# Gathers of a recommendation kernel: one pause ahead of arrival 16, or a pause each ahead of arrivals 16 and 17

## The reference

```
sparse_embed = emb_tables[field, x_sparse]           # 512 x 26 x 64
gram  = einsum('bik,bjk->bij', sparse_embed, sparse_embed)
inner = gram[:, iu, ju]                              # the 325 pairs i < j
dnn_in = concat([x_dense, sparse_embed.reshape(512, 1664), inner])   # 512 x 2002
h   = relu(dnn_in @ w1 + b1)                         # w1 is 2002 x 2002
out = sigmoid(h @ w2 + b2)                           # 512 x 1
```

## Time and profile before

| | us |
|---|---|
| median of 3 runs | 213.66 |
| lowest and highest | 212.72, 214.28 |
| the profiled execution's time | 214.66 |
| its span | 212.5 |
| TensorE busy | 201.6 (95% of the span) |
| VectorE busy | 148.6 (70%) |
| ScalarE busy | 129.3 (61%) |
| GpSimd busy | 129.4 (61%) |
| bytes moved | 39.00 MB, 184 GB/s in the mean |

### The profile page before, as it was taken

How to read it: one execution, slowest core, us unless ns; L and a number is a source line. 1 busy time by engine, 2 the same in 40 slices (tenths; PEclk the granted TensorE clock), 3 DMA queues, 4 the chain that set the end, 5 groups by cost and what they waited for, 6 DMA issues and landing times.

```text
span 212.5 us, 3900 instructions
## 1 busy us (share of the span) xinstructions
PE 201.6 (95%) x1340; PEld 161.4 (76%) x1340; DVE 148.6 (70%) x347; ACT 129.3 (61%) x256; POOL 129.4 (61%) x210
## 2 busy tenths in 40 slices
PE   8859999999999999999999799799999999999994
PEld 8834888877777878776887688588888877788882
DVE  3559457488937779879459796777587679773483
ACT  2657443479948939977338844679698558542201
POOL 4887888888787878218877878788788500000000
PEclk9997999999999999999999999999999999999999
DMA  5676999968484912326965667698975637223100
GB/s 153 188 226 201 305 327 344 323 203 281 119 291 125 299 51 63 86 56 169 325 217 178 196 180 189 185 329 299 325 213 161 207 98 212 87 35 63 32 0 0
DMA packets 15388, 39.00 MB, mean 184 GB/s; under 512 B 3881, under 2 KB 5281, under 8 KB 15369
## 3 DMA queue, kind: packets, MB, share of 16 engines
q1 hardware_dynamic: 11688, 35.27, 51.3%
q0 software_dynamic: 3328, 3.41, 7.6%
q10 hardware_dynamic: 353, 0.08, 0.2%
HBM read 37.71 MB, written 0.69 MB: 181 GB/s over the span
## 4 chain that ended last, share of the span: by engine, by line
PE 69%; POOL 15%; DMA 6%; issue 5%; DVE 3%; ACT 2%; DVEq 0%; POOLq 0%; ACTq 0%
PE slot L1079 20%; PE slot L1082 19%; PE slot L1085 19%; POOL E L823 13%; DMA E<-emb,row_idx 5%; PE slot L1039 4%; PE slot L1018 3%; POOL pace L831 2%; DVE G L977 2%; PE slot L1071 1%; PE slot L1069 1%; PE slot L1070 1%; ACT w_hi L847 1%; DMA x_idx<-idx 1%; DVE slot L1003 1%
## 5 line engine op out<-in xcount | busy, mean ns | idle before, releaser
L823 POOL DMA_INDIRECT E<-emb,row_idx x104 | 111.7, 1074 | 37.8 <-POOL pace L831 25.7
L929 DVE TENSOR_TENSOR w_lo<-w_raw,w_hi 128x500 fp32r<-128x500 f32 (+6 forms) x128 | 80.8, 671 | 13.2 <-ACT w_hi L847 12.5
L847 ACT CAST w_hi<-w_raw 128x1000 fp32r<-128x1000 f32 (+6 forms) x64 | 65.7, 1029 | 27.3 <-DMA w_raw<-w 15.4
L1079 PE MATMUL slot<-w_hi,x_hi 128*128 128x500 f32 (+5 forms) x236 | 75.0, 399 | 3.4 <-ACT x_hi L873 2.1
L1082 PE MATMUL slot<-w_lo,x_hi 128*128 128x500 f32 (+5 forms) x236 | 73.3, 390 | 2.3 <-DVE w_lo L929 2.2
L1085 PE MATMUL slot<-w_hi,x_lo 128*128 128x500 f32 (+5 forms) x236 | 72.7, 389 | 0.0
L1079 PEld LDWEIGHTS slot<-w_hi,x_hi 128*128 128x128 f32 (+2 forms) x236 | 43.0, 189 | 15.3 <-ACT x_hi L873 5.0
L1082 PEld LDWEIGHTS slot<-w_lo,x_hi 128*128 128x128 f32 (+2 forms) x236 | 44.5, 189 | 12.1 <-DVE w_lo L929 3.0
L1085 PEld LDWEIGHTS slot<-w_hi,x_lo 128*128 128x128 f32 (+2 forms) x236 | 44.4, 189 | 9.3 <-DVE x_lo L959 0.2
L878 ACT COPY ET<-T 32x128 f32<-32x128 f32 (+4 forms) x88 | 32.1, 364 | 2.0
L946 DVE STREAM_TRANSPOSE T<-E 128x256 f32<-128x256 f32 x24 | 10.6, 443 | 18.8 <-DMA E<-emb,row_idx 18.6
(11 more groups left out here) (39 smaller groups left out, 85.8 us busy)
## 6 DMA issues: line engine op xcount, KB each, us to landing
w_raw<-w SPq DMA_DIRECT2D x32, 501.0 KB, 4.7
w_raw<-w SPq DMA_DIRECT2D x32, 500.0 KB, 4.7
E<-emb,row_idx POOLq DMA_INDIRECT x104, 4.3
w_all<-w SPq DMA_DIRECT2D x1, 1001.0 KB, 6.9
gram_dram<-G SPq DMA_DIRECT2D x8, 84.5 KB
x_in<-gram_dram SPq DMA_DIRECT2D x8, 42.0 KB
x_in<-G SPq DMA_DIRECT2D x4, 58.5 KB
x_in<-G SPq DMA_DIRECT2D x4, 19.5 KB
```

Source lines behind the costliest of these rows:

```text
L823: nc.gpsimd.indirect_dma_start(out=E[:, k % ER, j, :], out_offset=None, in_=emb_rows, in_offset=bass.IndirectOffsetOnAxis(ap=row_idx[:, at ...
L847: nc.scalar.copy(w_parts(m)[0], w_source(m)).then_inc(w_hi_ready, 1)
L929: nc.vector.tensor_tensor(lo[:, cols], w_source(m)[:, cols], hi[:, cols].bitcast(F32), ALU.subtract)\
L1079: nc.tensor.matmul(acc[q], xh, hi[:, cols[q]], start=first, stop=False)
```

## The change

The condition of the pause is held in a table from arrivals to numbers of gram rounds. Arrival 16 waits for two rounds, arrival 17 for four. The same table is read in the plan (`gather`) and where GpSimd's instructions are written. Nothing else is edited; the lists of the engines come out of the plan.

```diff
-PAUSE, RESUME = 16, 4
+HELD_BACK = {16: 2, 17: 4}
...
-            if k == PAUSE:
-                if ("gram", RESUME - 1) not in done:
+            if k in HELD_BACK:
+                if ("gram", HELD_BACK[k] - 1) not in done:
                     return
-                pool_at = max(pool_at, done["gram", RESUME - 1] + HOP)
+                pool_at = max(pool_at, done["gram", HELD_BACK[k] - 1] + HOP)
...
-                if k == PAUSE:
-                    pool.wait_ge(gram_done, RESUME)
+                if k in HELD_BACK:
+                    pool.wait_ge(gram_done, HELD_BACK[k])
```

## The result

The changed kernel takes 214.94 us (median of 22 runs, 213.46 to 218.0), the kernel before 213.65 us (22 runs, 211.41 to 215.93). The ratio is 1.0063, with a 95% interval of 1.0039 to 1.0086. So the change costs about 1.3 us. My forecast was a gain of 1.4 us. The measured time lies inside the range given, and the sign is wrong; that it is inside is no merit of the mechanism, since the upper end of the range was made for rival C.

A forecast was written before the change was run, and what follows sets the result against it. TensorE, busy for 95% of the span, was taken as the bound, with 2.86 us of its gaps possibly due to late gathers. Only the 1.42 us stall counted: 213.66 − 1.42 = 212.2 us, range 210.4 to 215.0.

The forecast's parts named there:

- rival C: New VectorE and ScalarE orders lose what the stall gave; two turns cost 0.64 us or more each; 213.7 us, chance 0.12.
- Steps 1 and 2: On GpSimd, arrival 16's gathers start 7.9 us earlier without a pause; arrival 17 gets the pause, starting 6.3 us earlier.
- Step 3: On VectorE, turn 17 takes 16's place, turn 18 17's; turn 16 goes behind weight 29's low halves, 0.45 us.
- Step 4: TensorE's stall at 134.93 us goes, as arrival 21 comes earlier; 1.42 us gained, bounds 0 and 1.42.
- Step 5: TensorE's stalls at 115.76 and 118.27 us stay, VectorE held as before; value 0, bounds 1.44 gained, 0.6 lost.
- Step 6: Arrival 16's gathers move beside the first gram tiles' store and fetch, at DMA share 0.26; cost nothing.
- the rule: VectorE copies can lock GpSimd's shared port, slowing moved gathers some 2.5 us each, sum 0; the trace disagreed.
- Rivals L and D: L: VectorE's copies lock GpSimd, 213.7 us, chance 0.06; D: gathers delay gram tiles' store and fetch, 215.9 us, chance 0.11.
- my signs of being wrong: TensorE's or VectorE's order differing by more than one turn before 110 us, or a new stall of over a microsecond.

The follow-up runs named there:

- the exchange in the kernel before: Kernel before, with ScalarE's rounding of weight 38 moved just ahead of the x_hi of tile 3's small group, gathers as before: 216.7 us, ratio 1.012.
- weight 38 put back: Changed kernel with ScalarE's rounding of weight 38 moved behind the x_hi of tile 3's small group: 212.62 us against 214.05, ratio 0.9934.
- the old plan: Changed kernel's GpSimd waits, with the plan and every engine's list of the kernel before: 210.43 us, ratio 0.9835.

## Why the prediction was wrong, step by step

**Steps 1 and 2, right.** GpSimd has the one pause, and the later arrivals are about 6 us earlier: the last gather of arrival 21 starts at 122.12 us in place of 128.84, which is 5.5 us sooner when the 1.2 us of this execution's start are taken off.

**Step 3, right as far as it went.** Turn 17 took turn 16's place, turn 18 that of turn 17 (it even went one low half further up), and turn 16 stands behind the low halves of weight 29. I followed VectorE's list only, and took ScalarE's list as shifted in the same way. TensorE's own list changes too, from about 146 us on, which I had not foreseen; nothing here shows a price for it.

**Step 4, right.** The gap near 134 is gone. In the changed kernel alone that proves little, since TensorE comes there late, as in the run with the exchange in the kernel before. The runs with weight 38 put back and with the old plan have no gap there either, and TensorE is not late in them.

**Step 5, the step that failed.** It gave the gap near 118 a value of 0 with bounds of 1.44 gained and 0.6 lost. It measured 1.36 + 0.11 lost in the gap, and 1.55 behind it, 3.0 us in all. Its part on VectorE was right: VectorE is held until nearly the same moments by the turns of arrivals 17 and 18, and the copy to X24 comes 0.1 us later. Two things were missing. The first is the knock-on of the added turn: I costed its 0.45 us at nothing since VectorE has idle time at 105.68 on the chip, but the plan has no idle time there, and it is the plan that writes the lists. Half a microsecond in the plan changed the order of two pieces on another engine, and on the chip this was worth a load's landing and a rounding. The second is the clock: no term of my sum had it, although the mean granted clock of 0.992 before said that it had fallen somewhere, and that execution has the fall at 15 us, behind a gap of 2.17 us.

**Step 6 and the rule, right.** The four moved gathers took 0.95, 0.95, 0.95 and 1.32 us, beside VectorE's copies; the transfers beside the gram tiles cost nothing. Rivals L and D are out by the run with the old plan.

**The rivals.** C named the mechanism (an order that eats the gain), but priced it on VectorE, with two turns ahead of low halves of 0.64 us each; the price was 3.0 us, by one rounding on ScalarE and the clock behind it. It should have been the slower rival, with the clock in its price. Nor did my signs of being wrong cover what happened: I looked for a stall of over a microsecond at a place that had none, and this one grew at a place that had one.

Not settled: a part of the spread of single executions (the changed kernel's 22 runs lie over 4.5 us) is due to whether and how long the clock falls; the four longest of them have the mean granted clocks 0.975 to 0.983. I did not try to tell how long a gap has to be, and the 2.56 us without a fall say that this is not the whole of it. Open too are the 2.6 us of the exchange in the kernel before, and the gaps of 0.8 us at 106.90 and 109.90 in two of the runs with the new lists.

## What to carry to other kernels

When a change enters a planner's rules, its effect is two changes: what the chip does, and what lists come out. Try them apart, old lists with new waits and the reverse; here the new waits are worth −1.65% and the new lists +1.5%, and together they are +0.6%. And in the plan look at every engine behind an added piece, since 0.05 us there can exchange two pieces whose order is worth a microsecond on the chip.

Price a gap of TensorE with the clock that may fall behind it: here a gap that grew from 1.09 to 2.45 us cost not 1.4 but 2.9 us.

Gaps in a row on one chain don't add: removing an early one moves the wait to the next late datum, and adding one pays for the next.

## What the hardware showed that I had not expected

Gaps of 2.20, 2.45 and 2.52 us in the middle of dense work were each followed by three to four microseconds at the lower clock (starts of pairs 0.83 us apart in place of 0.46). It did not always begin at once: behind the gap of 2.20 us the first three pairs ran at the full clock. And it did not always come: behind the gap of 2.56 us at 14.00, in one of the same executions, the clock stayed at 1.00.
